# Attention probabilities scaled before their transposes on ScalarE, instead of the attention output scaled by a transposed row of reciprocal sums on VectorE

## The chip, the cores and the metric

The kernel is one program on one core of a Trainium2 chip. The metric is the device time of one execution in microseconds (us). Before the change three runs gave 1057.88, 1060.75 and 1061.19 us, median 1060.75. One more execution was profiled; it took 1055.73 us, of which 1053.9 us lie between its first and its last instruction (the span).

Engine names in the rows: PE is TensorE's matmul stream and PEld its weight loads, DVE is VectorE, ACT is ScalarE, POOL is GpSimd, SP issues DMAs. Each engine runs its own list of instructions in order and meets the others only at semaphores.

## The reference, cut to what matters

One transformer layer on 2048 tokens of width 512, in fp32: attention with a window of 256 keys, a LayerNorm, a feed-forward part with a shared expert and 8 routed ones, a second LayerNorm. The change touches the attention.

```python
q, k, v = jnp.split(hidden_states @ Wqkv, 3, axis=-1)
q = rmsnorm(q, q_norm_w); k = rmsnorm(k, k_norm_w)      # then split in 16 heads of 32, rope on both
mask = (q_idx >= k_idx) & (q_idx - k_idx <= WINDOW - 1)
scores = jnp.einsum('bqhd,bkhd->bhqk', q, k) * scale
scores = jnp.where(mask[None, None, :, :], scores, jnp.float32(-jnp.inf))
probs = jax.nn.softmax(scores, axis=-1)
o = jnp.einsum('bhqk,bkhd->bqhd', probs, v).reshape(b, s, h)
return o @ Wo
...
x = _layernorm(x + attention(x))
x = _layernorm(x + ffn(x))
```

The softmax divides every row of exp(score - max) by its sum. That division can be made on the probabilities, or, since the product with v is linear, on the output row of each head.

## The kernel before, in words

The attention works on 16 blocks of 128 tokens. A block s has four steps, one for each group g of four heads, so there are 64 steps with scores (and some more at the end for what trails behind). `steps()` lists them and every engine walks the same list in its own program: `tensor_program`, `scalar_program`, `vector_program`, `gpsimd_program`, `sync_program`. The order on each engine is the order in which its program is written; nothing reorders it.

What a step (s, g) does, with n the step before it (n = 4s + g - 1):

- TensorE: the scores of this step (L598: 12 matmuls into four PSUM banks `score_ps`); the transposes of the probabilities of the step before, `prob_transposes(n)` (L610: eight of them, four for the first pair of heads into `probT_ps0`, four for the second pair into `probT_ps1`); half a projection (six matmuls of 128x512), a "turn" (four transposes of one 128x512 tile, L584), the other half of the projection; the products with v of two steps back (`values(n-1)`, L626). The projection is q, k, v of the next block in steps g = 0, 1, 2 and the output projection Wo of the previous block in g = 3. What is turned is x1 of an older block (g = 0), `spread` (g = 1), q (g = 2) and k (g = 3). The turns write the same bank as the transposes of the first pair, so a turn comes after VectorE's copy of that pair.
- VectorE: mask and negated maximum of the first pair (L460, L464), copy of the transposed probabilities of the step before, first pair (L494), mask and maximum of the second pair, then what the step's projection and turn need: the weighting of q or k (L477), the low halves of split operands (`kT_lo`, `qT_lo`, `oT_lo`, `xT_lo`), the LayerNorm statistics, the residual sum `res` (L567, in g = 3).
- ScalarE: copy of the transposed probabilities of the step before, second pair (L344, `probT_out`, which waits for `probT_mm`, the end of both pairs' transposes); two exponentials of the first pair (L337, each also sums its row into `rsum`); the copy out of the step's turn (L421, L418, L363, L368); two exponentials of the second pair; then the square of q or k (L358) in g = 0 and 1, or the split of x and the copy of v (L350, L377) in g = 2.
- GpSimd: rotates q and k, multiplies the probabilities of the block's own keys by a mask (L272), and small pieces.

The sums' way in the kernel before: when block s-1 is done, VectorE in step (s, 0) takes the reciprocal of its 16 sums (L532) and spreads them over 512 columns (L534, tile `spread`); TensorE turns `spread` in step (s, 1) (L584); ScalarE copies the result to `oT` (L418); VectorE in step (s, 2) multiplies the attention output `oT_ps` by it (L523); ScalarE makes `oT_hi` (L410), VectorE `oT_lo` (L547), and the output projection of step (s, 3) uses both.

The probabilities' way: `exps` writes `prob[:, g % 2]`, and `prob_transposes(n)` one step later waits for `exp_made`.

After the attention comes the feed-forward part, which begins beside the last two blocks.

Of the kernel before, what the change touches and what calls it, by code (L numbers as in the profile page):

```python
# [10 lines left out]
P = 128  # L11
# [70 lines left out]
def attention_phase(nc, x, xT, Wqkv, q_w, k_w, Wo, trig, ident_in, masks_in, x1_dram, x1T, load_ahead):  # L82
# [3 lines left out]
    with ExitStack() as ctx:  # L86
# [56 lines left out]
        rrep_mm, wo_mm, x1T_mm = map(sem, ("rrep_mm", "wo_mm", "x1T_mm"))  # L143

        xT_hi_made, q_sq, k_sq, v_made, exp_made = map(sem, ("xT_hi_made", "q_sq", "k_sq", "v_made", "exp_made"))
        probT_act, rrep_made, oT_hi_made = map(sem, ("probT_act", "rrep_made", "oT_hi_made"))
# [3 lines left out]
        probT_dve, rinv_made, rinv_spread, oT_made, oT_lo_made = map(sem, ("probT_dve", "rinv_made", "rinv_spread", "oT_made", "oT_lo_made"))  # L150
# [169 lines left out]
        def scalar_program(act, beside):  # L320
# [18 lines left out]

            def probT_out(n):  # L340

                wait(act, probT_mm, 2 * n + 2)
                wait(act, pv_mm, n - 1)
                nc.scalar.copy(probT[:, n % 2, 2:4, 0:2, :], probT_ps[1][:, 0, :].rearrange("p (h w t) -> p h w t", h=2, w=2)).then_inc(probT_act, 1)  # L344
# [59 lines left out]
            for s, g in steps():  # L404
# [3 lines left out]
                if g == 2 and has(s - 1):  # L408
                    wait(act, oT_made, s)
                    nc.scalar.copy(oT_hi[:, :, :], tiled(oT[:, :])).then_inc(oT_hi_made, 1)  # L410
# [4 lines left out]
                if g == 1 and has(s - 1):  # L415
                    wait(act, rrep_mm, s)
                    wait(act, oT_lo_made, s - 1)
                    nc.scalar.copy(oT[:, :], turned_ps[:, 0, :]).then_inc(rrep_made, 1)  # L418
# [16 lines left out]
                if g == 2 and has(a):  # L435
                    take_v(a)
                beside(s, g)

        def vector_program(dve, beside):
# [78 lines left out]
            for s, g in steps():  # L518
                a, n = s + 1, 4 * s + g - 1
                if g == 2 and has(s - 1):  # L520
                    wait(dve, pv_mm, 4 * s)
                    wait(dve, rrep_made, s)
                    nc.vector.tensor_tensor(oT[:, :], oT_ps[:, 0, :], oT[:, :], ALU.mult).then_inc(oT_made, 1)  # L523
# [6 lines left out]
                if g == 0 and has(s - 1):  # L530
                    wait(dve, exp_made, NH * s)
                    nc.vector.reciprocal(rinv[:, :], rsum[:, (s - 1) % 2, :]).then_inc(rinv_made, 1)  # L532
                    wait(dve, rinv_made, s)
                    nc.vector.tensor_copy(spread[:, :].rearrange("p (h d) -> p h d", d=HD), rinv[:, :].unsqueeze(2).to_broadcast([P, NH, HD])).then_inc(rinv_spread, 1)  # L534
# [1212 lines left out]
```

## Time and profile before

| | |
|---|---|
| runs (three), median | 1057.88 to 1061.19 us, 1060.75 us |
| the profiled execution, its span | 1055.73 us, 1053.9 us |
| TensorE busy | 1026.3 us, 97% of the span |
| VectorE busy | 767.8 us, 73% |
| ScalarE busy | 639.3 us, 61% |
| GpSimd busy | 439.6 us, 42% |
| granted TensorE clock | 0.996 of full speed |
| chain that ended last | TensorE 92%, VectorE 2%, ScalarE 1%, GpSimd 1% |

The busy times are sums over stages with different limits. The attention fills about the first 400 us. Matmuls overlap, so a TensorE row's duration is longer than the time to the start of the next row; what a matmul costs is the distance between starts. The same holds on ScalarE and VectorE to a smaller degree: the next instruction starts some 0.1 us before the previous one's recorded end. An idle time in brackets stands at the instruction that ended it, with the engine and line that released it.

### The profile page before, as it was taken

What the parts mean: (1) busy time and instruction counts of PE and PEld (TensorE: products, weight loads), DVE (VectorE), ACT (ScalarE), POOL (GpSimd) and SP (SyncE); (2) the same over time, 40 slices, a digit from 0 to 9 for tenths busy, and PEclk for the clock granted to TensorE, in tenths of its full rate; (3) what the DMA queues carried; (4) which work ended last, traced back from release to release, by engine and by line L of the source; (5) the groups of instructions that cost most, each with busy time, mean ns of one, the idle gap of its engine ahead of it and who ended that gap; (6) DMA issues with size and microseconds to landing.
All of it is one profiled execution on the core that took longest, in us unless ns stands there. A gap on an engine that the chain in (4) does not pass through costs nothing.

```text
span 1053.9 us, 19775 instructions
## 1 busy us (share of the span) xinstructions
PE 1026.3 (97%) x7120; PEld 841.5 (80%) x7120; DVE 767.8 (73%) x1150; ACT 639.3 (61%) x1306; POOL 439.6 (42%) x540
## 2 busy tenths in 40 slices
PE   7999999999999999999999999999999999999995
PEld 4677777777777676888888888888888888888884
DVE  6878888888888875793767677676777777677374
ACT  5666666666666664443766666666666666766344
POOL 3688887888888731000122222222222222221173
PEclk9999999999999999999999999999999999999998
DMA  5111111111111126627699999999999999989563
GB/s 202 43 33 33 33 33 52 35 32 43 33 33 33 35 79 198 200 71 223 209 257 257 261 274 256 244 268 256 255 281 262 255 254 262 257 248 259 121 205 120
DMA packets 120981, 171.36 MB, mean 163 GB/s; under 512 B 10114, under 2 KB 63746, under 8 KB 120804
## 3 DMA queue, kind: packets, MB, share of 16 engines
q1 hardware_dynamic: 111856, 149.54, 45.0%
q0 software_dynamic: 8736, 20.45, 11.7%
q8 instruction: 58, 0.95, 0.4%
q14 instruction: 39, 0.32, 0.1%
q10 hardware_dynamic: 292, 0.10, 0.0%
HBM read 151.45 MB, written 23.07 MB: 166 GB/s over the span
## 4 chain that ended last, share of the span: by engine, by line
PE 92%; DVE 2%; ACT 1%; POOL 1%; issue 0%; POOLq 0%; ACTq 0%; DVEq 0%
PE probT_ps L610 6%; PE proj_ps L579 5%; PE proj_ps L577 5%; PE proj_ps L578 5%; PE oT_ps L626 5%; PE score_ps L598 4%; PE gate_ps L1573 4%; PE gate_ps L1575 4%; PE gate_ps L1574 4%; PE up_ps L1573 4%; PE up_ps L1575 4%; PE up_ps L1574 4%; PE down_ps L1608 4%; PE down_ps L1610 4%; PE down_ps L1609 4%; PE e_up_ps L1634 3%
## 5 line engine op out<-in xcount | busy, mean ns | idle before, releaser
L1031 POOL DMA_INDIRECT sum_dram<-rows,target_i x39 | 62.1, 1591 | 364.3 <-ACT rows L1139 364.3
L1415 DVE TENSOR_TENSOR e_lo<-e_raw,e_hi 128x1408 fp32r<-128x1408 f32 x78 | 126.7, 1624 | 49.0 <-ACT e_hi L1113 49.0
L1113 ACT CAST e_hi<-e_raw 128x1408 fp32r<-128x1408 f32 x78 | 107.5, 1379 | 52.4 <-PE e_up_ps L1645 52.4
L337 ACT ACTIVATE prob<-score_ps,nbias 128x256 f32<-128x256 f32 (+1 forms) x256 | 117.9, 470 | 4.5 <-DVE nbias L464 4.5
L272 POOL TENSOR_TENSOR probT<-probT,masks 128x256 f32<-128x256 f32 x128 | 92.6, 750 | 63.0 <-DVE probT L494 63.0
L1420 DVE TENSOR_TENSOR ed_lo<-ed_raw,ed_hi 128x1024 fp32r<-128x1024 f32 x39 | 47.8, 1225 | 77.5 <-ACT ed_hi L1121 51.0
L1037 POOL DMA_INDIRECT rows<-x_dram,token_i x39 | 53.4, 1369 | 94.8 <-DVE target_i L1382 65.4
L464 DVE TENSOR_REDUCE nbias<-score_ps 128x2 f32<-128x512 f32 (+1 forms) x128 | 86.3, 675 | 4.4
L344 ACT COPY probT<-probT_ps 128x512 f32<-128x512 f32 x64 | 37.5, 587 | 79.9 <-PE probT_ps L610 79.9
L577 PE MATMUL proj_ps<-wqkv_lo,xT_hi 128*128 128x512 f32 x180 | 78.1, 434 | 1.2 <-ACT squares L358 1.2
L1573 PE MATMUL gate_ps<-x_hi,gu_lo 128*128 128x512 f32 x180 | 72.6, 404 | 0.4 <-DVE gu_lo L1280 0.4
L579 PE MATMUL proj_ps<-wqkv_hi,xT_lo 128*128 128x512 f32 x180 | 71.2, 396 | 0.0
L1575 PE MATMUL gate_ps<-x_hi,gu_hi 128*128 128x512 f32 x180 | 70.8, 393 | 0.0
L1574 PE MATMUL gate_ps<-x_lo,gu_hi 128*128 128x512 f32 x180 | 70.6, 392 | 0.0
L578 PE MATMUL proj_ps<-wqkv_hi,xT_hi 128*128 128x512 f32 x180 | 70.5, 392 | 0.0
L1608 PE MATMUL down_ps<-wd_hi,h_lo 128*128 128x512 f32 x176 | 70.4, 400 | 0.0
L610 PE MATMUL probT_ps<-ident,prob 128*128 128x128 f32 x512 | 69.9, 280 | 0.0
L460 DVE COPY_PREDICATED score_ps<-masks,score_ps 128x256 f32<-128x256 int32 x112 | 47.3, 423 | 30.3 <-PE score_ps L598 30.2
L1573 PE MATMUL up_ps<-x_hi,gu_lo 128*128 128x512 f32 x172 | 69.1, 402 | 0.0
L1610 PE MATMUL down_ps<-wd_hi,h_hi 128*128 128x512 f32 x176 | 68.9, 392 | 0.0
L1609 PE MATMUL down_ps<-wd_lo,h_hi 128*128 128x512 f32 x176 | 68.5, 389 | 0.0
L1575 PE MATMUL up_ps<-x_hi,gu_hi 128*128 128x512 f32 x172 | 67.7, 393 | 0.0
(259 smaller groups left out, 2959.4 us busy)
## 6 DMA issues: line engine op xcount, KB each, us to landing
e_raw<-in_We_gu SPq DMA_DIRECT2D x78, 704.0 KB
ed_raw<-in_We_down SPq DMA_DIRECT2D x39, 512.0 KB, 5.3
raw_ring<-in_Ws_gu SPq DMA_DIRECT2D x58, 256.0 KB
wd_raw<-in_Ws_down SPq DMA_DIRECT2D x44, 256.0 KB, 6.3
gu_raw<-in_Ws_gu SPq DMA_DIRECT2D x30, 256.0 KB
ed_raw<-in_We_down SPq DMA_DIRECT2D x39, 192.0 KB, 6.8
xT_in<-in_xT SPq DMA_DIRECT2D x16, 256.0 KB, 2.7
x_in<-in_x SPq DMA_DIRECT2D x16, 256.0 KB, 3.1
```

What stands on the lines that cost most here:

```text
L337: nc.scalar.activation(prob[:, g % 2, h, seen], score_ps[:, h, seen], ACT.Exp, bias=nbias[:, s % 2, head:head + 1], scale=1.0, accum_out=r ...
L577: nc.tensor.matmul(out, l_hi[:, k, :], w_lo[:, k, :], start=(k == 0), stop=False)
L578: nc.tensor.matmul(out, l_hi[:, k, :], w_hi[:, k, :], start=False, stop=False)
L579: last = nc.tensor.matmul(out, l_lo[:, k, :], w_hi[:, k, :], start=False, stop=(k == KT - 1))
L610: last = nc.tensor.transpose(probT_ps[pair][:, 0, at:at + P], prob[:, n % 2, 2 * pair + h, w * P:(w + 1) * P], ident[:, :])
L1415: nc.vector.tensor_tensor(e_lo[:, part, :], raw_half(i, half), e_hi[:, part, :].bitcast(FP32), ALU.subtract).then_inc(e_lo_made, 1)
L1573: nc.tensor.matmul(o, gu_lo[:, n % 2, k, part], x_hi[tt % 2][:, k, :], start=(k == 0), stop=False)
L1574: nc.tensor.matmul(o, gu_hi[:, n % 2, k, part], x_lo[tt % 2][:, k, :], start=False, stop=False)
L1575: last = nc.tensor.matmul(o, gu_hi[:, n % 2, k, part], x_hi[tt % 2][:, k, :], start=False, stop=(k == KT - 1))
L1608: nc.tensor.matmul(down_ps[i][:, :], hl, wd_hi[:, n % 2, :], start=(u == 0), stop=False)
L1609: nc.tensor.matmul(down_ps[i][:, :], hh, wd_lo[:, n % 2, :], start=False, stop=False)
L1610: nc.tensor.matmul(down_ps[i][:, :], hh, wd_hi[:, n % 2, :], start=False, stop=(u == UN - 1)).then_inc(down_mm, 1)
```

## The change

The reciprocals are now taken group by group and applied to the probabilities. In step (s, g), at the end of its list, VectorE waits for the step's four exponentials and takes four reciprocals. At the end of its list ScalarE waits for these and multiplies each head's 128x256 probabilities (128x128 in block 0) by them in place, four instructions. The transposes wait for this product instead of for the exponentials. Gone are, once a block: the spread copy, its turn on TensorE, ScalarE's copy of the turn, VectorE's multiply of the attention output. `oT_hi` and `oT_lo` are now made from the PSUM bank `oT_ps` itself.

```diff
+            def norm_probs(s, g):
+                wait(act, rinv_made, 4 * s + g + 1)
+                seen = slice(0, 2 * P if s else P)
+                for h in range(4):
+                    head = 4 * g + h
+                    nc.scalar.activation(prob[:, g % 2, h, seen], prob[:, g % 2, h, seen], ACT.Identity, scale=rinv[:, head:head + 1]).then_inc(prob_normed, 1)
...
@@ scalar_program
                 if g == 2 and has(s - 1):
-                    wait(act, oT_made, s)
-                    nc.scalar.copy(oT_hi[:, :, :], tiled(oT[:, :])).then_inc(oT_hi_made, 1)
+                    wait(act, pv_mm, 4 * s)
+                    nc.scalar.copy(oT_hi[:, :, :], tiled(oT_ps[:, 0, :])).then_inc(oT_hi_made, 1)
...
-                if g == 1 and has(s - 1):
-                    wait(act, rrep_mm, s)
-                    wait(act, oT_lo_made, s - 1)
-                    nc.scalar.copy(oT[:, :], turned_ps[:, 0, :]).then_inc(rrep_made, 1)
...
                 if g == 2 and has(a):
                     take_v(a)
+                if has(s):
+                    norm_probs(s, g)
                 beside(s, g)
...
@@ vector_program
-                if g == 2 and has(s - 1):
-                    wait(dve, pv_mm, 4 * s)
-                    wait(dve, rrep_made, s)
-                    nc.vector.tensor_tensor(oT[:, :], oT_ps[:, 0, :], oT[:, :], ALU.mult).then_inc(oT_made, 1)
...
-                if g == 0 and has(s - 1):
-                    wait(dve, exp_made, NH * s)
-                    nc.vector.reciprocal(rinv[:, :], rsum[:, (s - 1) % 2, :]).then_inc(rinv_made, 1)
-                    wait(dve, rinv_made, s)
-                    nc.vector.tensor_copy(spread[:, :].rearrange("p (h d) -> p h d", d=HD), rinv[:, :].unsqueeze(2).to_broadcast([P, NH, HD])).then_inc(rinv_spread, 1)
...
-                    nc.vector.tensor_tensor(oT_lo[:, :, :], tiled(oT[:, :]), oT_hi[:, :, :].bitcast(FP32), ALU.subtract).then_inc(oT_lo_made, 1)
+                    nc.vector.tensor_tensor(oT_lo[:, :, :], tiled(oT_ps[:, 0, :]), oT_hi[:, :, :].bitcast(FP32), ALU.subtract).then_inc(oT_lo_made, 1)
...
+                if has(s):
+                    wait(dve, exp_made, NH * s + 4 * g + 4)
+                    nc.vector.reciprocal(rinv[:, 4 * g:4 * g + 4], rsum[:, s % 2, 4 * g:4 * g + 4]).then_inc(rinv_made, 1)
                 beside(s, g)
...
@@ tensor_program
             def prob_transposes(n):
                 for pair in range(2):
-                    wait(pe, exp_made, 4 * n + 2 * pair + 2)
+                    wait(pe, prob_normed, 4 * n + 2 * pair + 2)
...
             def values(n):
-                    wait(pe, oT_made, s)
+                    wait(pe, oT_lo_made, s)
...
-                if g == 1 and has(s - 1):
-                    wait(pe, rinv_spread, s)
-                    turned(spread).then_inc(rrep_mm, 1)
```

Two places show how the instructions stand now. The first is ScalarE in a step g = 0 in the middle of the attention, from the copy of the transposed probabilities to the same copy of the next step (`squares` is the square of q for its norm, `x1T` the turned x1). Before:

```order
L344 COPY probT<-probT_ps 128x2x256 [waits pv_mm,probT_mm]
L337 ACTIVATE prob,rsum<-score_ps,nbias 128x256 [waits maxed]
L337 ACTIVATE prob,rsum<-score_ps,nbias 128x256
L421 COPY x1T<-probT_ps 128x4x128 [waits x1T_mm]
L337 ACTIVATE prob,rsum<-score_ps,nbias 128x256 [waits maxed]
L337 ACTIVATE prob,rsum<-score_ps,nbias 128x256
L358 ACTIVATE squares,ssq<-proj_ps 128x512 [waits q_weighted]
L344 COPY probT<-probT_ps 128x2x256 [waits pv_mm,probT_mm]
```

And now, with the line numbers of the changed kernel:

```order
L352 COPY probT<-probT_ps 128x2x256 [waits pv_mm,probT_mm]
L337 ACTIVATE prob,rsum<-score_ps,nbias 128x256 [waits maxed]
L337 ACTIVATE prob,rsum<-score_ps,nbias 128x256
L425 COPY x1T<-probT_ps 128x4x128 [waits x1T_mm]
L337 ACTIVATE prob,rsum<-score_ps,nbias 128x256 [waits maxed]
L337 ACTIVATE prob,rsum<-score_ps,nbias 128x256
L366 ACTIVATE squares,ssq<-proj_ps 128x512 [waits q_weighted]
L346 ACTIVATE prob<-prob,rinv 128x256 [waits rinv_made]
L346 ACTIVATE prob<-prob,rinv 128x256 x3
L352 COPY probT<-probT_ps 128x2x256 [waits pv_mm,probT_mm]
```

The four products (L346) stand between the square and the next step's copy, and they wait for VectorE's reciprocals.

The second is VectorE in a step g = 3, from the second pair's maximum to the next step's mask (`res` is the residual sum). Before:

```order
L464 TENSOR_REDUCE nbias<-score_ps 128x2 [waits merged]
L488 TENSOR_TENSOR kT_lo<-probT_ps,kT_hi 128x4x128 [waits kT_hi_made]
L469 TENSOR_TENSOR xT_lo<-xT_in,xT_hi 128x512 [waits xT_hi_made]
L567 TENSOR_TENSOR res<-proj_ps,x_in 128x512 [waits x_loaded,x1_made,wo_mm]
L460 COPY_PREDICATED score_ps<-masks,score_ps 128x2x128 [waits score_mm]
```

And now:

```order
L470 TENSOR_REDUCE nbias<-score_ps 128x2 [waits merged]
L494 TENSOR_TENSOR kT_lo<-probT_ps,kT_hi 128x4x128 [waits kT_hi_made]
L475 TENSOR_TENSOR xT_lo<-xT_in,xT_hi 128x512 [waits xT_hi_made]
L564 TENSOR_TENSOR res<-proj_ps,x_in 128x512 [waits x_loaded,x1_made,wo_mm]
L567 RECIPROCAL rinv<-rsum 128x4 [waits exp_made]
L466 COPY_PREDICATED score_ps<-masks,score_ps 128x2x128 [waits score_mm]
```

The reciprocal (L567 of the changed kernel) stands behind the residual sum, which itself waits for the output projection on TensorE.

## Rows read from the trace of the kernel before

**Rows 1.** Two stretches: length; PE, PEld, DVE, ACT, POOL busy (x); clock; DMA share; GB/s.
```profile
15.00:20.00 5.00, 2.36 (x12) 1.53 (x11) 4.97 (x9) 2.82 (x6) 1.11 (x2) 1.00 0.31 93
60.00:340.00 280.00, 280.00 (x2921) 216.40 (x2910) 232.05 (x400) 182.06 (x569) 228.73 (x317) 1.00 0.12 37
```

**Rows 2.** Waits over 20:385 (us in total, times, longest).
```profile
ACT probT L344 <- PE probT_ps L610: 77.2, 59, 2.5
```

**Rows 3.** TensorE in time, 203:229 (start, us, instruction xcount, idle before).
```profile
205.88 0.47 PE L577 MATMUL proj_ps<-wqkv_lo,xT_hi 128*128 128x512 f32 x1
...
211.64 0.48 PE L577 MATMUL proj_ps<-wqkv_lo,xT_hi 128*128 128x512 f32 x1
...
213.12 0.60 PE L584 MATMUL probT_ps<-ident,spread 128*128 128x128 f32 x4
...
214.72 0.40 PE L579 MATMUL proj_ps<-wqkv_hi,xT_lo 128*128 128x512 f32 x1
...
217.42 0.48 PE L577 MATMUL proj_ps<-wqkv_lo,xT_hi 128*128 128x512 f32 x1
...
223.20 0.48 PE L577 MATMUL proj_ps<-wo_lo,oT_hi 128*128 128x512 f32 x1
...
228.97 0.47 PE L577 MATMUL proj_ps<-wqkv_lo,xT_hi 128*128 128x512 f32 x1
```

**Rows 4.** TensorE in time, 43:49, a projection with no turn inside.
```profile
45.13 0.48 PE L577 MATMUL proj_ps<-wqkv_lo,xT_hi 128*128 128x512 f32 x1
...
47.74 0.39 PE L579 MATMUL proj_ps<-wqkv_hi,xT_lo 128*128 128x512 f32 x1
```

**Rows 5.** ScalarE in time, the same 203:229.
```profile
206.16 0.59 ACT L344 COPY probT<-probT_ps 128x512 f32<-128x512 f32 x1 [2.44 <-PE probT_ps L610]
...
207.99 0.59 ACT L421 COPY x1T<-probT_ps 128x512 f32<-128x512 f32 x1 [0.32 <-PE probT_ps L584]
208.47 0.48 ACT L337 ACTIVATE prob<-score_ps,nbias 128x256 f32<-128x256 f32 x1
...
210.11 0.60 ACT L358 ACTIVATE squares<-proj_ps 128x512 f32<-128x512 f32 x1 [0.61 <-DVE qk L477]
210.60 0.19 ACT L358 ACTIVATION_READ_ACCUMULATOR squares<-proj_ps 128x1 f32 x1
...
221.43 0.60 ACT L377 COPY v_ring<-proj_ps 128x512 f32<-128x512 f32 x1
```

**Rows 6.** VectorE in time, the same 203:229.
```profile
203.44 0.68 DVE L469 TENSOR_TENSOR xT_lo<-xT_in,xT_hi 128x512 fp32r<-128x512 f32 x1
...
207.86 0.24 DVE L532 RECIPROCAL rinv<-rsum 128x16 f32<-128x16 f32 x1
...
209.42 0.66 DVE L477 TENSOR_TENSOR qk<-proj_ps,qw_b 128x512 f32<-128x512 f32 x1
...
226.54 1.22 DVE L469 TENSOR_TENSOR xT_lo<-xT_in,xT_hi 128x512 fp32r<-128x512 f32 x1
```

**Rows 7.** ScalarE's instructions by form, whole span (count, busy us, mean ns, idle).
```profile
L337 ACT ACTIVATE prob<-score_ps,nbias 128x256 f32<-128x256 f32 x240 | 112.1, 477 | 3.5 <-DVE nbias L464 3.5
...
L1149 ACT ACTIVATE x1T<-x1T,rstd_y 128x512 f32<-128x512 f32 x16 | 12.1, 807 | 4.7 <-POOL rstd_y L1062 4.7
L350 ACT CAST xT_hi<-xT_in 128x512 fp32r<-128x512 f32 x16 | 10.0, 622 | 0.8 <-DMA xT_in<-in_xT 0.8
...
L337 ACT ACTIVATE prob<-score_ps,nbias 128x128 f32<-128x128 f32 x16 | 5.8, 370 | 1.0 <-DVE nbias L464 1.0
...
L383 ACT ACTIVATE cs_rms<-cs,rms 128x64 f32<-128x64 f32 x2 | 0.7, 348 | 1.6 <-POOL rms L264 1.6
```

**Rows 8.** TensorE in time, 359:361, a turn that had to wait.
```profile
359.87 0.66 PE L584 MATMUL probT_ps<-ident,qk 128*128 128x128 f32 x4 [2.26 <-DVE probT L494]
360.28 0.47 PE L577 MATMUL proj_ps<-wqkv_lo,xT_hi 128*128 128x512 f32 x1
```

**Rows 9.** VectorE, the copy that this turn waited for.
```profile
359.13 0.68 DVE L494 COPY probT<-probT_ps 128x512 f32<-128x512 f32 x1
```

More of the change, by code:

```diff
@@ L142, in attention_phase @@
         score_mm, probT_mm, pv_mm = map(sem, ("score_mm", "probT_mm", "pv_mm"))
-        rrep_mm, wo_mm, x1T_mm = map(sem, ("rrep_mm", "wo_mm", "x1T_mm"))
+        wo_mm, x1T_mm = map(sem, ("wo_mm", "x1T_mm"))
         xT_hi_made, q_sq, k_sq, v_made, exp_made = map(sem, ("xT_hi_made", "q_sq", "k_sq", "v_made", "exp_made"))
-        probT_act, rrep_made, oT_hi_made = map(sem, ("probT_act", "rrep_made", "oT_hi_made"))
+        probT_act, prob_normed, oT_hi_made = map(sem, ("probT_act", "prob_normed", "oT_hi_made"))
         x1T_made, qT_hi_made, kT_hi_made = map(sem, ("x1T_made", "qT_hi_made", "kT_hi_made"))
         xT_lo_made, q_weighted, k_weighted, merged, maxed = map(sem, ("xT_lo_made", "q_weighted", "k_weighted", "merged", "maxed"))
-        probT_dve, rinv_made, rinv_spread, oT_made, oT_lo_made = map(sem, ("probT_dve", "rinv_made", "rinv_spread", "oT_made", "oT_lo_made"))
+        probT_dve, rinv_made, oT_lo_made = map(sem, ("probT_dve", "rinv_made", "oT_lo_made"))
         res_made, bn_made, mv_made, x1_made = map(sem, ("res_made", "bn_made", "mv_made", "x1_made"))
@@ L633, in turned_taken @@
                     wait(pe, x1T_made, min(s - 2, NB))
-                elif g == 1:
-                    wait(pe, rrep_made, min(s, NB))
                 elif g == 2:
                     wait(pe, qT_lo_made, min(s + 2, NB))
-                else:
+                elif g == 3:
                     wait(pe, kT_lo_made, min(s + 2, NB))
@@ L701, in tensor_program @@
                     project(*part, range(KT // 2))
-                if behind and has((s - 3, s - 1, a, a)[g]):
+                if behind and has((s - 3, -1, a, a)[g]):
                     wait(pe, probT_dve, n + 1)
@@ L722, in attention_phase @@
         carried.update(sync=sync_program, gpsimd=gpsimd_program, scalar=scalar_program, vector=vector_program, tensor=tensor_program,
-                       v_mm=v_mm, kT_mm=kT_mm, res_made=res_made, probT_act=probT_act, x1_stored=x1_stored, x1T_made=x1T_made, oT_made=oT_made, exp_made=exp_made)
+                       v_mm=v_mm, kT_mm=kT_mm, res_made=res_made, probT_act=probT_act, x1_stored=x1_stored, x1T_made=x1T_made, exp_made=exp_made)
 def constants():
```

## The prediction

> **What bounds the kernel now.** I read the busy times by stretch first, then the waits, then the three engines' timelines over one block, and last the instruction forms for durations.
>
> In 60:340 TensorE is busy for all of 280.00 us, and ScalarE for 182.06, so ScalarE is idle for 97.9 us [rows 1]. Most of ScalarE's idle time is one wait: its copy of the transposed probabilities waits for TensorE, 77.2 us in 59 waits over the attention [rows 2]. So the attention is bound by TensorE's instruction stream. One block takes 228.97 - 205.88 = 23.09 us and its four steps 5.76, 5.78, 5.78 and 5.77 us [rows 3]. I call t the moment in a step when the transposes of the probabilities are all issued and the first matmul of the projection starts: t = 205.88, 211.64, 217.42, 223.20 for g = 0 to 3. Everything below is an offset from t.
>
> **What goes away.** Once a block TensorE no longer turns `spread`. With the turn inside, the last matmul of the projection starts 214.72 - 211.64 = 3.08 us after the first [rows 3]; without one it is 47.74 - 45.13 = 2.61 [rows 4]. That is 0.47 us per block on the bound engine, 16 times: 7.5 us. VectorE's reciprocal, spread and multiply, and ScalarE's copy, lie beside TensorE's work, so as long as TensorE bounds the attention they bring nothing. They only shorten queues.
>
> **What is added, by kind.** ScalarE gets four multiplications of 128x256 in SBUF with a per-row scale, in each of the 64 steps. No row has this form exactly. The nearest is L383, the same operation and operands with 64 columns, 348 ns; a column costs (477 - 370)/128 = 0.84 ns by the two forms of L337; so 348 + 192 x 0.84 = 0.51 us [rows 7]. Back to back ScalarE starts the next instruction 0.11 us before a recorded end (207.99 + 0.59 against 208.47 [rows 5]), so four of them take 4 x 0.41 = 1.6 us of the engine and the last ends 3 x 0.41 + 0.51 = 1.74 us after the first has started. From below: a plain cast of 128x512 from SBUF takes 622 ns, so 0.41 us at 256 columns, and the last ends at 1.34. From above: the form with scale and bias rows, 807 ns at 512, so 0.59 us, and the last ends at 2.06 [rows 7]. I take 1.74, since its form is the same. VectorE gets 64 reciprocals of 4 columns; the row for 16 columns is 0.24 us [rows 6], and VectorE has 48 us idle in 60:340 [rows 1].
>
> By amount of work this would fit: 1.6 us in each of 48.5 steps is 80 us, into 97.9 us of idle. It is the waits that decide.
>
> **The new chain.** Before, the transposes of step n waited for exponentials that had ended a full scores block earlier. Now they wait for the products, which stand last in ScalarE's list of the step. And ScalarE's next list begins with the copy that waits for exactly these transposes. So there is a ring: transposes of n-1, ScalarE's whole list of the step, products, transposes of n. Its length has to be under 5.77 us or the ring, not TensorE's work, sets the step. The pieces:
>
> - From t to the start of the copy: 206.16 - 205.88 = 0.28 [rows 5, 3].
> - S, the offset at which the products can start. g = 0: the square starts at 210.11 - 205.88 = 4.23. It is released by VectorE's weighting at 209.42, which needs the whole projection, so it stays at this offset from t however late t is [rows 5, 6]. The next instruction can start 0.58 later: S = 4.81. The reciprocal is ready by then (weighting plus 0.24).
> - g = 1: the same with a projection shorter by 0.47: S = 4.34. The copy of the turn that goes was hidden beside the projection.
> - g = 2: ends with the copy of v at 221.43 - 217.42 = 4.01, 0.49 until the next: S = 4.50 [rows 5, 3]. The new place of the `oT_hi` cast (0.62 us, [rows 7] has the same form) is at the step's start, where ScalarE has to wait for the transposes anyway; free.
> - g = 3: here VectorE is last. Its list is `xT_lo`, then `res`, then the reciprocal. `xT_lo` starts at 226.54 - 223.20 = 3.34 [rows 6, 3]. It takes 0.68 or 1.22 us in the two rows; the long one lies beside GpSimd's multiplies, which in the stretched step will be over. With the short one: 3.34 + 0.60 + 0.60 + 0.24 + 0.03: S = 4.81; with the long one 5.35.
> - From the last product's end to TensorE: 0.06, as from the end of VectorE's copy, 359.13 + 0.68, to 359.87. Four transposes that had to wait then take 360.28 - 359.87 = 0.41 until the next matmul [rows 8, 9].
>
> So the new step is S + 1.74 + 0.06 + 0.41 = S + 2.21, that is 7.02, 6.55, 6.71 and 7.02: 27.30 us per block against 23.09, +4.2. All are above the 5.77 (5.30 for g = 1) that TensorE needs, so the ring holds in every step and the 7.5 us saved on TensorE vanish in it: TensorE stands still for about 1.2 us before the second pair's transposes. What is late next to the products is nothing else: GpSimd's rotations and VectorE's lists gain time with the longer step, and VectorE's new wait for the exponentials (they end at about 3.6) holds up only masks whose scores come at about 5.0.
>
> Sixteen blocks: 16 x 4.21 = 67 us. The first block has shorter products but also shorter steps, and the last two have feed-forward work in the gaps, some of it on ScalarE behind the products; I leave them at the same rate. The feed-forward part proper is unchanged. Against the profiled execution: 1055.7 + 67 = 1123 us. The median of the runs is 5 us above this execution, which gives 1128; I say 1125.
>
> **A rule that speaks against it.** The products use an identity between exponentials, and TensorE would wait through any reload of ScalarE's tables. The trace of before has the identity of L383 and the exponentials of L337 in one stretch of ScalarE's list with no load between them. The Trainium skill, "ScalarE: Activation LUTs", section "Table sets: the hidden batching unit", says that cheap functions such as identity are in every set; by that rule the price is zero, as I have it. If it did not hold, its "about 2.66 us" for a switch, an estimate of two per step, would be +340 us.
>
> **The rivals.**
>
> 1. *The idle time swallows the products: faster.* ScalarE has 97.9 us idle for 80 us of products. If the waits inside its list (for the turn, for the weighting) shrink when it falls behind, the ring could fit into 5.77 us, and TensorE stays the bound and gives back its turns: 1055.7 - 7.5 = 1048 us. The point from which it decides is S + 2.21 < 5.77, S < 3.56. Against it: the weighting cannot come before the projection ends, which alone puts S at 4.3 or more. Chance 0.05.
> 2. *The ring is longer.* Products of 0.59 us (+0.32 x 64 = 20 us) and the long `xT_lo` in every block (+0.54 x 16 = 9): 1055.7 + 67 + 29 = 1152 us. For it: `xT_lo` is long in one of the two rows. Chance 0.10.
> 3. *The ring is shorter*, with products of 0.41 us: -0.40 x 64 = -26 us, 1097 us. Chance 0.10.
> 4. *TensorE's clock falls*, since the engine now pauses in each step. Against it: in 15:20 TensorE was busy for 2.36 of 5.00 us and the granted clock stayed at 1.00, 2.4 GHz [rows 1]; the new pauses are 1.2 us in 7. At the lower level TensorE's 5.3 to 5.8 us of a step would double, well over the ring: about +4.8 x 64 = +310 us if it lasted through the attention. The Trainium skill, "TensorE: Matmul & The Clock Gate", section "The HAM clock gate (the "warmup" mystery)", says that idle time brings the gate back to the lower level; by that rule such a fall is possible, and the trace has idle stretches of half the time without one. Chance 0.02.
>
> My forecast has the rest, 0.73. Its own range is 1112 to 1138. The range for 8 in 10 takes in rivals 2 and 3 in part: 1098 to 1148. Under 0.3% (3 us) a measurement of this kernel can tell nothing from no change. Faster by more: rival 1, 0.05. Within: 0.02, for a ring that fits only just. Slower: 0.93.
>
> **What would show it.** In the changed kernel's profile: TensorE waits before L610 with ScalarE's product line as releaser, some 60 times or more, 1.0 to 1.5 us each; TensorE busy in a mid-attention stretch falls to about 0.8; the distance between equal places of two blocks is 27.3 us; ScalarE's product lasts 0.51 us; no added table load; the granted clock stays at 1.00; the feed-forward part has its old length. I am wrong if ScalarE's copy (L352) still waits mostly for TensorE's matmuls with no wait of TensorE on the products (rival 1), if the product has another duration (rivals 2, 3), or if the last block's hand-over to the feed-forward part takes more than some 10 us of its own.

## The result

Four runs of the changed kernel gave a median of 1134.15 us, from 1132.86 us upwards; the kernel before gave 1059.80 us beside them. The ratio is 1.0702, 95% interval 1.0682 to 1.0722. One of the four took 1310.9 us, at a mean TensorE clock of 0.75; the median counts it (1133.23 us without it), the ratio and the traces below don't. The profiled execution of the changed kernel took 1135.07 us, its span is 1133.3 us. By medians the change costs 74 us; the two profiled executions are 79 apart, since the one of the kernel before was faster than its median.

Where the 79.4 us between the two spans are. The marks are the first matmul of the projection in step (1, 0) and in step (14, 0), the first gate matmul and the first down matmul of the feed-forward part:

| stretch | before | changed | difference | as predicted |
|---|---|---|---|---|
| start to step (1, 0) | 45.13 | 52.12 | +7.0 | +4.2 |
| 13 blocks | 299.30 | 352.32 | +53.0 | +54.7 |
| block 14, to the first gate matmul | 26.18 | 34.25 | +8.1 | +4.2 |
| from there to the first down matmul | 29.72 | 37.59 | +7.9 | +4.2 |
| the rest | 653.57 | 657.02 | +3.5 | 0 |

The changed kernel's page begins with the busy time of each engine, its share and its instructions, and then the granted clock in 40 slices:

```profile
PE 1048.4 (93%) x7056; PEld 845.3 (75%) x7056; DVE 745.1 (66%) x1166; ACT 729.8 (64%) x1546; POOL 432.4 (38%) x540
...
PEclk9899999999999999989999999999999999999998
```

Two stretches of it, with the columns of [rows 1]. TensorE, busy for all of 280.00 us there before, is now busy for 244.68:

```profile
60.00:340.00 280.00, 244.68 (x2427) 179.77 (x2425) 181.52 (x350) 214.87 (x644) 191.76 (x271) 1.00 0.10 31
...
420.00:425.00 5.00, 2.41 (x8) 2.12 (x9) 4.77 (x8) 2.27 (x8) 4.11 (x5) 0.74 0.00 0
440.00:445.00 5.00, 5.00 (x40) 3.64 (x38) 2.11 (x5) 1.98 (x8) 3.54 (x6) 0.71 0.00 0
```

Its waits over 20:470, as in [rows 2]. TensorE and its weight loads, which had no such wait, now stand before the transposes L610. "issue" names no engine; in the timeline below such a wait ends when ScalarE's products do, so these are the same wait (the first transpose of the block shown starts at 240.61 us, the second product has ended at 240.51, the fourth at 241.31):

```profile
PEld probT_ps L610 <- ACT prob L346: 44.9, 79, 2.4
PEld probT_ps L610 <- issue: 42.8, 45, 1.5
...
ACT probT L352 <- PE probT_ps L610: 37.1, 59, 1.5
PE probT_ps L610 <- issue: 29.8, 43, 1.2
```

TensorE over one block, to be read beside [rows 3]. The projections start at 234.87 (g = 3), 241.78, 248.75, 255.30 and 261.97, so the steps are 6.91, 6.97, 6.55 and 6.67 us, and the block 27.10 instead of 23.09. The eight transposes span 1.41 us, with a pause between the pairs in it:

```profile
234.87 0.48 PE L577 MATMUL proj_ps<-wo_lo,oT_hi 128*128 128x512 f32 x1
...
240.61 1.41 PE L610 MATMUL probT_ps<-ident,prob 128*128 128x128 f32 x8 [0.75 <-issue]
241.78 0.47 PE L577 MATMUL proj_ps<-wqkv_lo,xT_hi 128*128 128x512 f32 x1
...
248.75 0.48 PE L577 MATMUL proj_ps<-wqkv_lo,xT_hi 128*128 128x512 f32 x1
...
254.09 1.45 PE L610 MATMUL probT_ps<-ident,prob 128*128 128x128 f32 x8 [0.84 <-ACT prob L346]
255.30 0.47 PE L577 MATMUL proj_ps<-wqkv_lo,xT_hi 128*128 128x512 f32 x1
...
261.97 0.48 PE L577 MATMUL proj_ps<-wo_lo,oT_hi 128*128 128x512 f32 x1
```

ScalarE in the same block, which answers to [rows 5]. The products stand last in each step; in g = 3 they wait for the reciprocal, in g = 0 the square before them waits for VectorE's weighting:

```profile
239.61 1.71 ACT L346 ACTIVATE prob<-prob,rinv 128x256 f32<-128x256 f32 x4 [1.12 <-DVE rinv L567]
242.06 0.59 ACT L352 COPY probT<-probT_ps 128x512 f32<-128x512 f32 x1 [0.75 <-PE probT_ps L610]
...
246.00 0.60 ACT L366 ACTIVATE squares<-proj_ps 128x512 f32<-128x512 f32 x1 [0.61 <-DVE qk L483]
...
246.59 1.69 ACT L346 ACTIVATE prob<-prob,rinv 128x256 f32<-128x256 f32 x4
...
253.15 1.69 ACT L346 ACTIVATE prob<-prob,rinv 128x256 f32<-128x256 f32 x4
...
259.78 1.72 ACT L346 ACTIVATE prob<-prob,rinv 128x256 f32<-128x256 f32 x4
```

### The profile page after: what moved, and what is told of

Same layout as the page of the kernel before. It is cut to its first block, busy times and chain, and to the rows that moved or that the text cites. A ratio compares the mean times of both kernels' runs of the same rounds, so it can differ in the third digit from the quotient of the medians.

```text
span 1133.3 us, 19855 instructions
## 1 busy us (share of the span) xinstructions
PE 1048.4 (93%) x7056; PEld 845.3 (75%) x7056; DVE 745.1 (66%) x1166; ACT 729.8 (64%) x1546; POOL 432.4 (38%) x540
## 4 chain that ended last, share of the span: by engine, by line
PE 73%; ACT 13%; DVE 7%; issue 4%; DMA 1%; SPq 0%; POOL 0%; ACTq 0%; POOLq 0%; DVEq 0%
ACT prob L346 8%; PE proj_ps L579 4%; PE proj_ps L577 4%; PE proj_ps L578 4%; PE probT_ps L610 4%; PE up_ps L1568 3%; PE gate_ps L1568 3%; PE up_ps L1570 3%; PE up_ps L1569 3%; PE gate_ps L1570 3%; PE gate_ps L1569 3%; PE down_ps L1603 3%; PE down_ps L1605 3%; PE down_ps L1604 3%; PE e_up_ps L1629 3%
## 5 line engine op out<-in xcount | busy, mean ns | idle before, releaser
L272 POOL TENSOR_TENSOR probT<-probT,masks 128x256 f32<-128x256 f32 x128 | 91.9, 738 | 136.1 <-DVE probT L500 128.5
L610 PE MATMUL probT_ps<-ident,prob 128*128 128x128 f32 x512 | 83.6, 288 | 54.5 <-issue 29.8
L610 PEld LDWEIGHTS probT_ps<-ident,prob 128*128 128x128 f32 x512 | 55.1, 143 | 87.8 <-ACT prob L346 44.9
L346 ACT ACTIVATE prob<-prob,rinv 128x256 f32<-128x256 f32 (+1 forms) x256 | 107.2, 494 | 18.3 <-DVE rinv L567 18.3
```

The source lines that it names most:

```text
L346: nc.scalar.activation(prob[:, g % 2, h, seen], prob[:, g % 2, h, seen], ACT.Identity, scale=rinv[:, head:head + 1]).then_inc(prob_normed, 1)
L610: last = nc.tensor.transpose(probT_ps[pair][:, 0, at:at + P], prob[:, n % 2, 2 * pair + h, w * P:(w + 1) * P], ident[:, :])
```

## The experiments

Mean length of the four steps of a block, each from one projection's first matmul to the next, between 60 and 330 us of every profile. A step is named by the g at its start. The g = 0 column holds one step without a turn, (2, 0), in every kernel; it is some 0.5 us shorter (6.51 in the changed kernel, 6.96 or 6.97 in the other g = 0 steps). Each ratio is to the kernel before, run beside that kernel. Runs 6, 8 and 11 change only the last two blocks; their steps are those of the changed kernel, of early products and of products aside, within 0.02. It is the table by which most runs are read:

| kernel | g=3 | g=0 | g=1 | g=2 | median us | ratio to before |
|---|---|---|---|---|---|---|
| before | 5.79 | 5.73 | 5.77 | 5.77 | | |
| changed | 6.91 | 6.92 | 6.56 | 6.67 | 1134.15 | 1.0702 [1.0682, 1.0722] |
| products on 2 columns | 6.15 | 6.17 | 5.78 | 5.91 | 1081.96 | 1.0222 [1.0200, 1.0244] |
| products aside | 5.91 | 5.73 | 5.30 | 5.77 | 1069.34 | 1.0105 [1.0082, 1.0128] |
| early products | 6.05 | 6.12 | 6.20 | 6.18 | 1090.95 | 1.0303 [1.0276, 1.0330] |
| no division | 5.90 | 5.73 | 5.30 | 5.77 | 1053.85 | 0.9962 [0.9947, 0.9977] |
| turn put back | 6.92 | 6.92 | 7.03 | 6.66 | 1141.46 | 1.0756 [1.0738, 1.0775] |
| half and half | 5.84 | 6.06 | 6.63 | 7.14 | 1102.63 | 1.0395 [1.0376, 1.0415] |
| early, edge steps | 5.84 | 6.05 | 6.21 | 6.18 | 1085.30 | 1.0235 [1.0218, 1.0252] |
| early, middle steps | 6.05 | 6.12 | 6.50 | 7.13 | 1101.58 | 1.0389 [1.0371, 1.0406] |
| half and half, accumulator | 6.11 | 6.27 | 5.67 | 6.17 | 1082.40 | 1.0197 [1.0178, 1.0215] |

**1. Products on two columns.**

```diff
-nc.scalar.activation(prob[:, g % 2, h, seen], prob[:, g % 2, h, seen], ACT.Identity, scale=...)
+nc.scalar.activation(prob[:, g % 2, h, 0:2], prob[:, g % 2, h, 0:2], ACT.Identity, scale=...)
```

> Edit: the changed kernel with each product on two columns instead of 256 (it leaves the rest of the softmax division out; v is scaled by 1/64 to keep the values in range). Order, waits and instruction count stay. Ring theory: a step lasts S + (3 starts + 1 duration of a product) + 0.47, with S of 4.81, 4.34, 4.50, 4.81 for g = 0 to 3. A product of two columns lasts 0.30 us (348 ns at 64 columns less 62 x 0.84), starts 0.20 apart, so the last ends at 0.90: steps of 6.18, 5.71, 5.87, 6.18, a block of 23.9 us against 27.1 measured in the changed kernel, 16 x 3.2 = 51 us less than 1134: 1083 us. Rival (the engine's sum of work decides): with 0.8 instead of 1.6 us of products per step ScalarE has idle time to spare and the kernel falls to 1050 us. Rival (TensorE's clock does the harm): hardly any fall, 1110 or more, because the pauses stay.

Measured 1081.96 us, expected 1083. All waits and all products are there as in the changed kernel, only short: 0.285 us each (median), four in 0.84 to 0.86 instead of 1.69 to 1.72. The kernel leaves the rest of the division out, as runs 2, 4 and 11 do. Steps fall by 0.75 to 0.78 us, and stay above those of the kernel without any division (run 4). So the order of waits costs even where the products cost little, and their length adds to it.

**2. Products aside**, the full work at the same place, written where nobody reads:

```diff
-nc.scalar.activation(prob[:, g % 2, h, seen], prob[...], ACT.Identity, scale=...)
+nc.scalar.activation(aside(s, h), prob[...], ACT.Identity, scale=...)
...
-                    wait(pe, prob_normed, 4 * n + 2 * pair + 2)
+                    wait(pe, exp_made, 4 * n + 2 * pair + 2)
```

> Edit: the changed kernel with all four full products at the same place in ScalarE's list, but written to tiles that nobody reads; the transposes wait for the exponentials again (it leaves the softmax division out of the result; v scaled by 1/64). Ring theory: the ring is open, TensorE bounds the attention again and lacks its 16 turns: 1060 - 7.5 = 1052 us, ScalarE's list running up to 0.6 us late without anybody noticing. Rival (the sum of ScalarE's work decides): the time stays near 1134, at least over 1100 us.

Measured 1069.34 us, expected 1052. In the steady blocks the theory holds: ScalarE is busy for 248.47 of 280 us and TensorE for 279.25:

```profile
60.00:340.00 280.00, 279.25 (x2915) 214.28 (x2913) 219.32 (x417) 248.47 (x764) 227.91 (x320) 1.00 0.12 37
```

The steps are those of the kernel without any division (run 4). Of the 17 us between the two, 14 lie right behind the steady blocks: block 14 takes 31.45 us instead of 25.51, the way from the first gate matmul to the first down matmul 37.54 instead of 29.45. The granted clock was 0.95 and 0.91 in these two stretches, 1.00 without division, so a part of the 14 us is clock. I had left this part out, and runs 6 and 11 take it up.

**3. Early products**, ahead of the square, the split of x and the next block's work, with VectorE's reciprocals moved forward too:

```diff
                 if has(s):
                     exps(s, g, 1)
+                if g == 2 and has(a):
+                    take_v(a)
+                if has(s):
+                    norm_probs(s, g)
...
                     square(a, 1, k_weighted, k_sq)
-                if g == 2 and has(a):
-                    take_v(a)
-                if has(s):
-                    norm_probs(s, g)
                 beside(s, g)
```

> Edit: the changed kernel with the reciprocal ahead of the weighting (g = 0), of xT_lo and res (g = 3), and the products right behind the second pair's exponentials (g = 2: behind the copy of v), ahead of the square and the split of x. Full computation. Ring theory: S falls to 3.95, 3.87, 4.00, 3.88, steps of 6.16, 6.08, 6.21, 6.09, a block of 24.5 to 24.7 us: 16 x 2.4 = 39 us less, 1095 us. Rival (sum of work): no change, 1134.

Measured 1090.95 us, expected 1095. Nothing but the place in two engines' lists changed (g = 2 keeps the copy of v in front of the products), and 43 us of the 74 went. All four steps now have nearly one length, 6.05 to 6.20.

**4. No division**: the kernel before without reciprocals, spread, turn, copy and multiply. It shows what TensorE's own work takes in a step, but for g = 3.

> Edit: the kernel before with the whole way of the sums left out (no reciprocal, spread, turn, copy, multiply: it leaves the softmax division out; v scaled by 1/64). What the removed part is worth by itself. All theories: TensorE bound, 16 x 0.47 = 7.5 us less than before: 1052 us. If it were 1060, the turns had been hidden.

Measured 1053.85 us, ratio 0.9962: some 4 us gained, not 7.5. Step g = 1 gives the predicted 0.47 us, but g = 3 gets 0.11 longer on average. In 5 of the blocks 2 to 12 its turn of k starts 1.69 to 1.77 us after the first matmul of the projection instead of 1.48, 0.14 or 0.15 us behind the end of GpSimd's rotation of k. These steps take 6.02 to 6.10 us, the others 5.78 or 5.79. The prediction's 7.5 us was too much, in part by what this wait gives back.

**5. The turn put back on TensorE**, in the changed kernel, read by nobody:

```diff
-                if behind and has((s - 3, -1, a, a)[g]):
+                if behind and has((s - 3, s - 1, a, a)[g]):
                     wait(pe, probT_dve, n + 1)
...
+                if g == 1 and has(s - 1):
+                    turned(spread)
```

> Edit: the changed kernel with the removed turn put back on TensorE in every step g = 1 (four transposes of a tile of ones into the same bank; nobody reads them). Full computation. Ring theory: the turn makes the projection 0.47 us longer, so the weighting of k, the square and the products come 0.47 later: 15 to 16 x 0.47 = 7.0 to 7.5 us more than the changed kernel, 1141. Rival (TensorE pauses 1.2 us in each step, so it has room for a turn): no change, 1134.

Measured 1141.46 us, as expected: step g = 1 goes from 6.56 to 7.03, the others stay. In a kernel whose TensorE idles in every step, 0.47 us of matmul still cost 0.47 us, since they delay the projection's end, and by it the weighting, the square and the products.

**6. Feed-forward work ahead of the products in the last two blocks.**

```diff
-                if has(s):
+                if has(s) and s < NB - 2:
                     norm_probs(s, g)
                 beside(s, g)
+                if has(s) and s >= NB - 2:
+                    norm_probs(s, g)
```

> Edit: the changed kernel with, in blocks 14 and 15 alone, ScalarE's feed-forward casts ahead of the products instead of behind. Full computation. The extra 8 us between block 14 and the feed-forward part, if they come from casts that start 1.6 us late and hold up VectorE and the first gate matmuls: in (14, 1) and (14, 2) about 2 us less, before the first gate 2.6 less, some given back in block 15 because the products wait now: 1134 - 4 = 1130. Rival (the lower clock of these stretches is the cause): no change, 1134.

Measured 1123.35 us, ratio 1.0592 [1.0574, 1.0610], 11 us less than the changed kernel and 7 better than I expected. Block 14 takes 28.41 instead of 34.25 us, the next stretch 32.87 instead of 37.59. The rival expectation, the clock, isn't ruled out as a part: the granted clock of the two stretches was 0.95 and 0.91 in the changed kernel and 1.00 and 0.95 here. If TensorE had bounded them throughout, that is 34.25 x 0.05 + 37.59 x 0.09 = 5.1 us against 32.87 x 0.05 = 1.6, so at most some 3.5 of the 10.6 us gained there are clock (an estimate from these figures). What the products delay there is seen in the changed kernel, on ScalarE, VectorE and TensorE:

```profile
415.81 1.69 ACT L346 ACTIVATE prob<-prob,rinv 128x256 f32<-128x256 f32 x4
417.40 1.13 ACT L1083 CAST x_hi<-x1T 128x512 fp32r<-128x512 f32 x2
```

```profile
418.04 2.84 DVE L1271 TENSOR_TENSOR x_lo<-x1T,x_hi 128x512 fp32r<-128x512 f32 x2 [2.83 <-ACT x_hi L1083]
420.80 0.42 DVE L466 COPY_PREDICATED score_ps<-masks,score_ps 128x256 f32<-128x256 int32 x1
421.25 0.69 DVE L470 TENSOR_REDUCE nbias<-score_ps 128x2 f32<-128x512 f32 x1
421.86 0.68 DVE L500 COPY probT<-probT_ps 128x512 f32<-128x512 f32 x1
```

```profile
422.59 1.11 PE L584 MATMUL probT_ps<-ident,qk 128*128 128x128 f32 x4 [3.00 <-DVE probT L500]
...
438.69 0.50 PE L1568 MATMUL gate_ps<-x_hi,gu_lo 128*128 128x512 f32 x1 [2.06 <-DVE gu_lo L1275]
```

The feed-forward split `x_hi` stands behind the products in ScalarE's list. VectorE stands 2.83 us waiting for it, in the middle of its own list. Behind that are the next step's masks and the copy L500, and TensorE waits 3.00 us for the copy. The kernel before has a wait of this kind too, 2.26 us [rows 8].

**7. Half and half**: early products, the first pair's on VectorE.

```diff
+                    for h in range(2):
...
+                        nc.vector.tensor_scalar(prob[:, g % 2, h, seen], prob[:, g % 2, h, seen], rinv[:, head:head + 1], None, ALU.mult).then_inc(pair_normed, 1)
...
-                for h in range(4):
+                for h in range(2, 4):
```

> Edit: the early placement of the earlier run, and VectorE makes the first pair's two products right behind its reciprocals; ScalarE makes two; the LayerNorm's scaling of x1 moves behind the weighting of k in g = 1. Full computation. Ring theory: S of 3.9 to 4.0 + 0.41 + 0.51 + 0.47 = 5.3 to 5.4 us, under the 5.77 (5.30 in g = 1) that TensorE needs: TensorE bounds the attention, a block of 22.6 to 23.0 us against 23.1 before; with some 5 us of hand-over 1050 + 7 = 1057, that is level with the kernel before. Rival (VectorE, now with two products and two reciprocals' latency per step, becomes the bound): a block above 24 us, 1080 or more.

Measured 1102.63 us, expected 1057: slower than with all products on ScalarE, as the rival had it. Steps g = 3 and 0 became shorter than in run 3, g = 1 and 2 longer. VectorE in g = 0, 1 and 2, and GpSimd in the last two (two products in a row make one line):

```profile
232.69 0.67 DVE L510 TENSOR_SCALAR prob<-prob,rinv 128x256 f32<-128x256 f32 x2
...
238.61 2.02 DVE L510 TENSOR_SCALAR prob<-prob,rinv 128x256 f32<-128x256 f32 x2
...
245.66 2.09 DVE L510 TENSOR_SCALAR prob<-prob,rinv 128x256 f32<-128x256 f32 x2
```

```profile
239.22 1.26 POOL L204 TENSOR_TENSOR qk<-rot_a,rot_b 128x512 f32<-128x512 f32 x1
...
246.33 1.27 POOL L204 TENSOR_TENSOR qk<-rot_a,rot_b 128x512 f32<-128x512 f32 x1
```

Two products take 0.67 us in g = 0, where the GpSimd instruction beside them ends 0.25 us after their start, and 2.02 or 2.09 beside its rotations. These end at 240.63 and 247.75, some 0.15 us after a rotation has ended (240.48 and 247.60). This is so for every such product. Of those that start between 60 and 340 us of this run, 64 start while a GpSimd instruction runs (or up to 0.02 us before one begins), and each ends 0.14 or 0.15 us after that instruction. The other 22 take 0.35 or 0.36 us. The next runs test what this costs.

**8. Early products, and behind the feed-forward work in the last two blocks**: the edits of runs 3 and 6 together.

> The kernel with early products, and in the last two blocks the products stand behind the feed-forward work in ScalarE's list. Theory: the ring's rate and the hand-over are two separate costs that add. Moving the products behind saved 11 us on the changed kernel, in block 14 and in the stretch up to the first down product; here the steady blocks keep 24.5 us and the hand-over gives the same 11: 1091 - 11 = 1080 us. Rival: the early products already stand ahead of everything in the step, so the last blocks are bound by VectorE's and ScalarE's lists as a whole and moving them gives under 4 us: 1087 to 1091.

Measured 1087.70 us, ratio 1.0258 [1.0241, 1.0276] against 1.0303 [1.0276, 1.0330]. That is 3.3 us by the medians and 4.8 by the ratios, nearer to the rival (under 4) than to the 11: the two costs don't simply add. In the trace block 14 gains 1.6 us and the next stretch 4.8, but the profiled execution of run 3 was its slowest (1096.99 us), with a clock of 0.86 in that stretch against 0.95 here, so most of the 4.8 can be clock.

**9 and 10. VectorE's share only in steps g = 0 and 3, or only in g = 1 and 2.** Both also have the edit of run 8.

```diff
-                    for h in range(2):
+                    for h in range(2 if g in (0, 3) else 0):
```

The mirror has `(1, 2)` in place of `(0, 3)`, and ScalarE makes the products that are left.

> As the run before (early products, last two blocks behind the feed-forward work), but VectorE makes the products of the first pair of heads in steps g = 0 and 3, in which GpSimd does no rotation. Theory (VectorE's products are held up by GpSimd's two-input instructions, and by nothing else): all products of VectorE take 0.35 us each, ScalarE's list is 0.8 us shorter in two of four steps, and TensorE's waits in those steps go: 2 x 0.5 us x 16 = -16 us, 1080 - 16 = 1064 us. Rival: what the half-and-half kernel lost came from VectorE's list being too long whatever GpSimd does; then this kernel is no faster than the run before, 1080 us or more.

> The mirror of the run before: the same number of products on VectorE, but in steps g = 1 and 2, beside GpSimd's rotations of q and k. Theory: two products take 1.7 to 2.1 us there instead of 0.65, as in the half-and-half kernel, the transposes of the first pair wait for them by some 1.2 us, and the kernel is 2 x 1.2 x 16 = 38 us slower than its mirror: 1100 us. Rival (the length of VectorE's list alone counts, which is the same in both): the two are within 8 us of each other.

Measured 1085.30 and 1101.58 us, expected 1064 and 1100. The durations are close to the theory. VectorE's products over 60:340 in run 9 (count, then least, median and longest ns):

```profile
L512 DVE TENSOR_SCALAR prob<-prob,rinv x44: 345/353/541, 73.5 to 322.6; 128x256 f32<-128x256 f32 x44
```

The same in run 10:

```profile
L512 DVE TENSOR_SCALAR prob<-prob,rinv x44: 364/1122/1432, 59.7 to 324.9; 128x256 f32<-128x256 f32 x44
```

In run 9 half of them run beside a GpSimd instruction that is no rotation (L314 or L280) and take up to 0.54. In run 10 all 43 that start in this stretch start beside one, and each ends 0.14 to 0.16 us after it, as in run 7.

The sizes are not as expected. The mirror is 16 us slower, not 38: the steps g = 1 and 2 grow by 0.29 and 0.95, and g = 3 and 0, now without VectorE's help, by 0.21 and 0.07. That is more than the 8 us of its rival, so the length of VectorE's list alone is not the cause; that its own number, 1100, came out is luck, since the run that it was counted from was 21 us off. And run 9 is only 2.4 us faster than run 8, which their intervals don't separate: in g = 3 and 0 the early kernel was 0.15 and 0.39 us above the 5.90 and 5.73 of run 4, not the 0.5 each that I had put down, and 0.32 stays in g = 0. By time alone run 9's own rival (1080 us or more) stands.

**11. Products aside, and behind the feed-forward work in the last two blocks**: runs 2 and 6 together.

> The kernel whose products are made in full but that nobody reads (v scaled by 1/64, softmax division left out), now with the products of the last two blocks behind the feed-forward work. Theory: what that kernel had over the one without any sums (1069 against 1054) was ScalarE's feed-forward work, with products in front of it in the last two blocks: most of it goes, 1069 - 11 = 1058 us. Rival: it is the extra work of ScalarE itself, wherever it stands: 1067 us or more.

Measured 1055.19 us, expected 1058, ratio 0.9946 [0.9930, 0.9963], no slower than the kernel without any division. So 256 products on ScalarE, 240 of them of 256 columns, cost nothing by their amount. They cost by who waits for them: TensorE in the steady blocks, feed-forward splits in the last two.

**12. Half and half, with an accumulator** (the sum goes to a tile that nobody reads). Otherwise it is run 7:

```diff
-... rinv[:, head:head + 1], None, ALU.mult)
+... rinv[:, head:head + 1], 0.0, ALU.mult, ALU.add, accum_out=unused[:, head:head + 1])
```

> The half-and-half kernel (early products, VectorE makes the first pair's products in every step), with one thing changed: VectorE's products also write out an accumulator, which nobody reads. Rows so far: the plain form took 0.35 us in steps 0 and 3 and 1.12 us (median) in steps 1 and 2, beside GpSimd's rotations. Theory: it is the plain form of this instruction that is held until GpSimd's running instruction ends, not any instruction of VectorE; the form with an accumulator is not held, and takes about 0.42 us, as the masks of the same size do (estimate), in all four steps. Then steps 1 and 2, which were 6.63 and 7.14 us against 5.84 and 6.05 for the others, come down to about 6.0 each: -1.8 us per block, 16 times -29: 1103 - 29 = 1074 us. The Trainium skill, 'SBUF — State Buffer', lists tensor_scalar among the operations that can take the port pair shared with GpSimd, and excepts the form that also writes out its accumulator. Rival: GpSimd holds up VectorE in any form that reads SBUF; then the products keep their 1.1 us and the kernel its time, 1100 us or more.

Measured 1082.40 us, expected 1074. VectorE's products over 60:340, in all four steps:

```profile
L511 DVE TENSOR_SCALAR_CACHE_REDUCE prob<-prob,rinv x92: 471/478/481, 64.8 to 337.3; 128x256 f32<-128x256 f32 x92
```

The form does more work and takes 478 ns instead of 350, and no instance is held up: 471 to 481 in all 92, in the same steps where the plain form took up to 1433. Steps g = 1 and 2 fall by 0.96 and 0.97 us, g = 3 and 0 grow by 0.27 and 0.21 from the slower form. The Trainium skill, "SBUF — State Buffer", section "Who interferes with whom", has this: plain tensor_scalar from SBUF to SBUF can take the port pair shared with GpSimd, the accumulating form does not, and the second to come is blocked until the first instruction ends. The trace agrees: without an accumulator up to 1433 ns, ending 0.14 to 0.15 us after GpSimd's instruction, and with one at most 481. This kernel is the fastest of the variants that still divide by the sums, and none of these is faster than the kernel before.

## Why the prediction was right, and where it was off

**The ring.** It is what sets the attention now. The predicted steps from g = 3, 0, 1, 2 were 7.02, 7.02, 6.55 and 6.71, the measured ones 6.91, 6.92 (6.97 without the short one), 6.56 and 6.67; a block grows by 4.08 us where 4.21 were predicted. The terms: S was 4.81, 4.34, 4.50 and 4.81 for g = 0 to 3, and the trace has 246.59 - 241.78 = 4.81, 253.15 - 248.75 = 4.40, 259.78 - 255.30 = 4.48 and 239.61 - 234.87 = 4.74. Four products take 1.69 to 1.72 us, predicted 1.74. (The sums of the products use an overlap of 0.10 where the row gives 0.11; that is 0.03 us for four.) From their end to the next projection it is 248.75 - 248.28 = 0.47, predicted 0.06 + 0.41. The product's duration answers to the estimate from [rows 7], 0.51 us:

```profile
L346 ACT ACTIVATE prob<-prob,rinv 128x256 f32<-128x256 f32 x188 | 80.0, 502 | 13.4 <-DVE rinv L567 13.4
```

Runs 1, 3 and 5 each change one piece of the ring and the step moves with it; run 2 opens the ring, and the step falls to that of run 4. The waits before L610 that name the product line are there, 79 of them, but with 44.9 / 79 = 0.57 us each on average and not 1.0 to 1.5; the rest stands under "issue".

**The short duration of `xT_lo`.** Taking it was right, and for the reason given. Between 60 and 340 us of the changed kernel all ten take 0.68 us, and no GpSimd instruction runs beside any of them. Before, twelve took 0.68 to 1.29, and the seven of 1.22 or more are those that start within 0.06 us of the start of a GpSimd multiply (L272). VectorE's whole scaling of x moved in the same way: 1102 ns on average before, 557 in the changed kernel, 1424 with early products, where it falls on the rotations. The kernel before and the changed one, both over 60:340:

```profile
L544 DVE TENSOR_SCALAR x<-res,mv,rstd 128x512 f32<-128x512 f32 x12 | 13.2, 1102 | 0.0
```

```profile
L541 DVE TENSOR_SCALAR x<-res,mv,rstd 128x512 f32<-128x512 f32 x10 | 5.6, 557 | 0.0
```

**"The last two have feed-forward work in the gaps", left at the same rate.** This is the term that was mis-sized most. Block 14 and the stretch behind it cost 16.0 us instead of 8.4. Run 6 shows the cause: products standing in front of splits that other engines need; moving them back gives 11 us. A part of the 16.0, at most some 5 us by the estimate under run 6, is TensorE's lower clock in these stretches. No run parts the waits from the clock that fell with them. I had named over 10 us of its own for the hand-over as what would refute me; over the 8.4 of the ring it is 7.6, or 11.1 with the 3.5 us behind the first down matmul, so this came close.

**The first block, left at the same rate.** It cost 7.0 instead of 4.2. Its granted clock was 0.92 over the 52.12 us, and 1.00 in the 45.13 before. If TensorE had bounded it throughout, that is 52.12 x 0.08 = 4.2 us (an estimate), enough for the 2.8 too much; I made no run on it alone, and the cause stays open.

**"The feed-forward part proper is unchanged", "the granted clock stays at 1.00".** The first holds for most of that part. The second holds in the steady blocks, but not around them: the mean over the changed kernel is 0.985, against 0.996 before. The 3.5 us lie in a lower clock: in the first 100 us behind the first down matmul TensorE is busy throughout, with a clock of 0.97 and 497 matmuls. Before it was 1.00 and 511. First the changed kernel, then the one before:

```profile
476.28:576.28 100.00, 100.00 (x497) 81.23 (x494) 62.96 (x145) 35.13 (x50) 3.47 (x11) 0.97 0.54 170
```

```profile
400.33:500.33 100.00, 100.00 (x511) 81.28 (x508) 66.29 (x150) 38.91 (x56) 3.47 (x11) 1.00 0.57 181
```

Run 8 has 1.00 there and takes 653.45 us from that mark to its end, like the kernel before (653.57). So these 3.5 us are not the products' own work.

**"The 7.5 us saved on TensorE vanish in it"** (the ring). This was wrong in its wording. The saving was 0.36 us per block in a kernel bound by TensorE (run 4), and inside the ring the missing turn is worth 0.47 (run 5). My own S for g = 1 had it already.

**"TensorE stands still for about 1.2 us before the second pair's transposes."** The sum was right, the place was not: 0.75 us before the first pair and about 0.3 within the eight. The busy share in mid-attention is 0.87 and not 0.8; the pause within the eight counts in part as busy, since the rows of the matmuls overlap it.

**The rule on table loads.** It cost nothing, as forecast: the changed kernel has four table loads, as before, one at 1.5 us and three in the feed-forward part, 1.28 us each, and none in the attention.

In all, 67 us were predicted and 79 measured between the two profiled executions, 74 between the medians. The steady blocks came out 1.7 lower, and the first block, the hand-over and the lower clock behind it gave 2.8, 7.6 and 3.5 more. By the estimates above up to 4.2 and 5.1 us of the first two stretches may be clock as well. It isn't all of it: run 6 gains 10.6 us in block 14 and the next stretch, and at least some 7 of them are no clock. So the ring came out term by term. What the prediction had no term for is the order of the lists in the last two blocks, and short falls of the clock around the steady blocks; its rival on the clock was for the whole attention.

## What to carry to other kernels

When work is moved between an engine's output and another engine's wait, add up the loop of waits, from one transpose through the whole in-order list to the next, before comparing idle time with added work: here 80 us fit into 98 us of idle and still cost 74. Then ask who is queued behind the moved instruction in every stretch, not only in the steady one. Where VectorE and GpSimd both work on SBUF, the form of VectorE's instruction can matter more than its length.

## What the runs showed of the hardware

VectorE's plain multiply of 128x256 from SBUF to SBUF took 0.35 us alone. When it started beside a GpSimd instruction, as 107 did in runs 7 and 10 between 60 and 340 us, it ended 0.14 to 0.16 us after that instruction, and took up to 1.43. With an accumulator it took 0.48 in all 92 cases of run 12.

The granted clock fell in short stretches, not throughout. In 420:425 of the changed kernel it was 0.74, in the stretch of the 3.00 us pause, and in 440:445 0.71, behind a pause of 2.06 us. At the start it was 0.69 in 20:25, after a stretch (15:20, at 0.96) in which TensorE was busy for 2.38 of 5.00 us. The kernel before had 2.36 of 5.00 in that stretch [rows 1] and kept 1.00 in 20:25, and it also kept it behind its pause of 2.26 us [rows 8]. The fall at the start is not the products' doing alone: the kernel without any division had 0.96 over its first 45.73 us. The changed kernel first, then the one before:

```profile
20.00:25.00 5.00, 4.95 (x27) 3.31 (x25) 3.93 (x6) 1.35 (x3) 0.10 (x1) 0.69 0.00 0
```

```profile
20.00:25.00 5.00, 4.19 (x28) 2.65 (x27) 4.27 (x8) 1.69 (x3) 0.64 (x1) 1.00 0.00 0
...
360.00:365.00 5.00, 5.00 (x58) 3.88 (x59) 4.43 (x8) 3.27 (x11) 4.92 (x6) 1.00 0.01 3
```

In mid-attention, with some 1.1 us of waiting in each step (6.77 us on average, where the kernel without any division needs 5.68), it stayed at 1.00. What decides between these cases stays open.
